# Latent scores begin with the latents' own tile and their weighing is spread; in the 16-head attention a key item goes ahead of the turned maxima, and ScalarE issues four of the key moves

## The reference, cut to what matters

```python
# L1 and L2: 16 heads of 8, one batch element at a time (L1 with biases and a mask on the 1500 keys)
scores = einsum('bhqd,bhkd->bhqk', q, k) / sqrt(8)
out = einsum('bhqk,bhkd->bhqd', softmax(scores), v) @ Wo.T
# L3: 8 heads of 64; keys and values come from the context AND the 56 latents
kv = concatenate([layer_norm(context), layer_norm(latents)], axis=1) @ Wkv     # 1500 + 56 rows
sim = einsum('bhid,bhjd->bhij', l2norm(q) * q_scale, l2norm(k) * k_scale) * 8
sim = where(mask, sim, max_neg)                # the mask is on the 1500 context rows alone
out = layer_norm(einsum('bhij,bhjd->bhid', softmax(sim), v) @ Wo)
```

## Time and profile before

| what | us |
|---|---|
| median of three executions | 4443.74 |
| lowest and highest of them | 4441.89, 4443.81 |
| the profiled execution, its own time | 4445.88 |
| its span, first to last instruction | 4443.8 |
| TensorE busy in the span | 3737.9 |
| VectorE, ScalarE, GpSimd busy | 2632.0, 2039.1, 1119.3 |

### The profile page before, as it was taken

One profiled execution on the slowest core, in us unless ns is written; L12 is line 12 of the kernel. 1 busy time (PEld: TensorE's weight loads), 2 busy tenths in 40 slices (PEclk: granted clock), 3 DMA queues, 4 the chain that ended last, 5 costly groups with the idle time before them and its releaser, 6 DMA issues. The chain is left out here.

```text
span 4443.8 us, 97631 instructions
## 1 busy us (share of the span) xinstructions
PE 3737.9 (84%) x40750; PEld 2568.5 (58%) x40750; DVE 2632.0 (59%) x3696; ACT 2039.1 (46%) x3827; POOL 1119.3 (25%) x1043
## 2 busy tenths in 40 slices
PE   7789678888888799588888887255999999999988
PEld 4454357776777544377777775132666666666654
DVE  5634356666666233466666663433777777777751
ACT  3300035555555100255555553212777777777643
POOL 0000122222221100322222221200555555555530
PEclk8889889999999799799999998566999999999989
DMA  7800165555553000444444440000000000000000
GB/s 217 255 20 0 57 168 150 146 146 146 146 146 96 39 0 0 122 118 121 116 121 119 118 122 8 0 13 21 14 22 22 21 22 22 22 22 22 22 1 23
DMA packets 107986, 329.21 MB, mean 74 GB/s; under 512 B 54151, under 2 KB 55247, under 8 KB 107023
## 3 DMA queue, kind: packets, MB, share of 16 engines
q1 hardware_dynamic: 107567, 323.20, 27.2%
HBM read 168.20 MB, written 7.00 MB: 39 GB/s over the span
## 5 line engine op out<-in xcount | busy, mean ns | idle before, releaser
L1758 POOL TENSOR_TENSOR l_S<-l_S,l_shift 125x448 f32<-125x448 f32 (+1 forms) x416 | 461.1, 1143 | 278.4 <-ACT l_shift L1988 275.9
L1179 ACT ACTIVATE L2a_probs<-ps 125x448 f32<-125x448 f32 x768 | 383.2, 544 | 191.1 <-PE ps L1089 177.4
L1179 ACT ACTIVATE L1a_probs<-ps 125x448 f32<-125x448 f32 x768 | 383.3, 544 | 190.7 <-PE ps L1089 177.1
L1212 DVE TENSOR_REDUCE L2a_chunk_max<-ps 112x1 f32<-112x1000 f32 x256 | 300.8, 1197 | 166.8 <-PE ps L1052 166.4
L1212 DVE TENSOR_REDUCE L1a_chunk_max<-ps 112x1 f32<-112x1000 f32 x256 | 300.8, 1197 | 159.0 <-PE ps L1052 158.4
L1969 ACT ACTIVATE ctx_stats<-ps 125x512 f32<-125x512 f32 (+1 forms) x416 | 248.0, 596 | 216.6 <-PE ps L1816 205.4
L1867 PE MATMUL ps<-l_S,l_z 125*128 125x448 f32 x768 | 342.7, 543 | 0.0
L2059 DVE SCALAR_TENSOR_TENSOR l_S<-ps,l_neg_cols,l_inv_norms 125x448 f32<-125x448 f32 x384 | 258.5, 681 | 117.1 <-PE ps L1836 116.0
L2034 DVE TENSOR_REDUCE l_norms<-ctx_stats 125x8 f32<-125x512 f32 (+1 forms) x416 | 268.9, 676 | 82.6 <-ACT ctx_stats L1969 82.2
L1052 PE MATMUL ps<-L1a_keys,L1a_queries 98*112 98x500 f32 x768 | 261.8, 423 | 55.9 <-DVE L1a_k_full L1199 22.0
L1089 PE MATMUL ps<-L1a_queries,L1a_keys 100*125 100x224 f32 x1536 | 307.1, 299 | 0.4 <-ACT L1a_probs L1179 0.4
(11 more groups left out here) (407 smaller groups left out, 7646.8 us busy)
## 6 DMA issues: line engine op xcount, KB each, us to landing
L1a_keys<-L1a_k_hi SPq DMA_DIRECT2D x256, 187.5 KB
L2a_keys<-L2a_k_hi SPq DMA_DIRECT2D x256, 187.5 KB, 3.7
a_ctx_T<-in_ctx_T SPq DMA_DIRECT2D x32, 750.0 KB, 11.2
xn<-L_valid SPq DMA_DIRECT2D x32, 750.0 KB, 7.8
L1a_ctx_T<-in_ctx_T SPq DMA_DIRECT2D x32, 750.0 KB, 6.2
L1a_keys<-L1a_k_lo SPq DMA_DIRECT2D x128, 187.5 KB
L2a_ctx_T<-in_ctx_T SPq DMA_DIRECT2D x32, 750.0 KB, 6.5
L2a_keys<-L2a_k_lo SPq DMA_DIRECT2D x128, 187.5 KB, 4.1
```

Of the source, the lines that this page charges most:

```text
L1179: nc.scalar.activation(probs[t % NPR][:, h * HQ // 2:(h + 1) * HQ // 2], s.ps[0:KP, i % 3, 0:HQ // 2], ACT.Exp).then_inc(probs_made, 1)
L1212: ins = nc.vector.tensor_reduce(chunk_max[:, n, 0:1], product, AX.XY, ALU.max)
L1758: nc.gpsimd.tensor_tensor(S[b % 2][0:r, t, :], S[b % 2][0:r, t, :], shift[0:r, :], ALU.add)\
```

## The change

The diff, cut to its core:

```diff
@@ attention_16_heads
-    step_items[10] += [("turn", 1, 0), ("keys", 3, 0)]
-    step_items[11].append(("keys", 3, 1))
+    step_items[10].append(("keys", 3, 0))
+    step_items[11] += [("turn", 1, 0), ("keys", 3, 1)]
@@ move_keys, SyncE
-                sp.wait_ge(k_lo_made, b * 2 + 2)
-                for g in range(G):
-                    sp.dma_start(keys[b % NKB][GR:2 * GR, g, :].bitcast(F32),
-                                 k_lo[g * GR:(g + 1) * GR, :].bitcast(F32)).then_inc(keys_moved, 16)
+                if b < 2:
+                    sp.wait_ge(k_lo_made, b * 2 + 2)
+                    for g in range(G):
...
@@ ScalarE
+            def move_remainders(b):
+                if b >= NKB:
+                    act.wait_ge(scores_made, (b - NKB + 1) * KT * 2)
+                act.wait_ge(k_lo_made, b * 2 + 2)
+                for g in range(G):
+                    act.dma_start(keys[b % NKB][GR:2 * GR, g, :].bitcast(F32),
+                                  k_lo[g * GR:(g + 1) * GR, :].bitcast(F32)).then_inc(keys_moved, 16)
...
+                    if t == 1 and b + 2 < B:
+                        move_remainders(b + 2)
@@ attention_latents, TensorE
+        SCORED = [KT] + list(range(KT))
...
-                for t in range(T):
+                for i in range(T):
                     if b + 1 < B:
-                        score_product(b + 1, t)
-                    if b >= 0 and t + LEAD < KT:
-                        weigh(b, t + LEAD)
+                        score_product(b + 1, i)
+                    later = [LEAD + (i + k) * (KT - LEAD) // T for k in range(2)]
+                    if b >= 0 and later[1] > later[0]:
+                        weigh(b, later[0])
@@ attention_latents, VectorE
+            def raise_by_latents(b):
+                dve.wait_ge(topped, b * NTOP + 2)
+                nc.vector.tensor_tensor(top[0:SQ, 1, :], top[0:SQ, 1, :], S[b % 2][0:SQ, KT, :], ALU.max).then_inc(topped, 1)
+
             def join_tops(b):
-                dve.wait_ge(S_made, b * T + T)
-                dve.wait_ge(topped, b * NTOP + NTOP - 2)
-                nc.vector.tensor_tensor(top[0:SQ, 1, :], top[0:SQ, 1, :], S[b % 2][0:SQ, KT, :], ALU.max).then_inc(topped, 1)
                 dve.wait_ge(topped, b * NTOP + NTOP - 1)
...
-                    for t in range(T):
-                        scale_scores(b + 1, t)
-                        if t == 1 and b >= 1:
+                    for i in range(T):
+                        if i == KT and b + 2 < B:
+                            center_latents(b + 2)
+                        scale_scores(b + 1, i)
+                        if i == 1 and b >= 1:
                             take_output(b - 1)
-                        if t == 11 and b + 2 < B:
-                            center_latents(b + 2)
-                        if t >= 4 and t % 2 == 0:
-                            raise_top(b + 1, t - 2)
+                        if i >= 5 and i % 2 == 1:
+                            raise_top(b + 1, i - 3)
+                        if i == 8:
+                            raise_by_latents(b + 1)
+                    raise_top(b + 1, KT - 2)
                     join_tops(b + 1)
```

More of the change, by code:

```diff
@@ L949, in move_keys @@
                                      k_hi[g * GR:(g + 1) * GR, :].bitcast(F32)).then_inc(keys_moved, 16)
-                sp.wait_ge(k_lo_made, b * 2 + 2)
-                for g in range(G):
-                    sp.dma_start(keys[b % NKB][GR:2 * GR, g, :].bitcast(F32),
-                                 k_lo[g * GR:(g + 1) * GR, :].bitcast(F32)).then_inc(keys_moved, 16)
+                if b < 2:
+                    sp.wait_ge(k_lo_made, b * 2 + 2)
+                    for g in range(G):
+                        sp.dma_start(keys[b % NKB][GR:2 * GR, g, :].bitcast(F32),
+                                     k_lo[g * GR:(g + 1) * GR, :].bitcast(F32)).then_inc(keys_moved, 16)
             def move_maxima(b):
@@ L1714, in attention_latents @@
         NTOP = KT // 2 + 1
+        RAISED = {2: 0, 4: 1, 6: 3, 8: 4, 10: 5}
+        SCORED = [KT] + list(range(KT))
         def rows(t):
@@ L1826, in queries_through_keys, with score_product @@
                 mm.then_inc(G_made, 1)
-            def score_product(b, t):
-                if t == 0:
+            def score_product(b, i):
+                t = SCORED[i]
+                if i == 0:
                     pe.wait_ge(G_lo_made, b + 1)
-                if b * T + t >= 2:
-                    pe.wait_ge(S_made, b * T + max(t - 1, 0))
-                out = s.ps[0:rows(t), 2 + t % 2, 0:HQ3]
+                if b * T + i >= 2:
+                    pe.wait_ge(S_made, b * T + max(i - 1, 0))
+                out = s.ps[0:rows(t), 2 + i % 2, 0:HQ3]
                 nc.tensor.matmul(out, tile_of(b, t, 0), G_hi[:, :], start=True, stop=False)
@@ L1925, in _ @@
                             project_out(b - 1)
-                for t in range(T):
+                for i in range(T):
                     if b + 1 < B:
-                        score_product(b + 1, t)
-                    if b >= 0 and t + LEAD < KT:
-                        weigh(b, t + LEAD)
-                    if b + 2 < B and 7 <= t < 7 + NG:
-                        turn_context(b + 2, t - 7)
-                    elif b + 2 < B and t == 7 + NG:
+                        score_product(b + 1, i)
+                    later = [LEAD + (i + k) * (KT - LEAD) // T for k in range(2)]
+                    if b >= 0 and later[1] > later[0]:
+                        weigh(b, later[0])
+                    if b + 2 < B and 7 <= i < 7 + NG:
+                        turn_context(b + 2, i - 7)
+                    elif b + 2 < B and i == 7 + NG:
                         turn_latents(b + 2)
@@ L2047, in take_queries_lo, with scale_scores @@
                     .then_inc(G_lo_made, 1)
-            def scale_scores(b, t):
+            def scale_scores(b, i):
+                t = SCORED[i]
                 r = rows(t)
-                dve.wait_ge(raw_made, b * T + t + 1)
-                if t == 0 and b >= 2:
+                dve.wait_ge(raw_made, b * T + i + 1)
+                if i == 0 and b >= 2:
                     dve.wait_ge(sums_made, b - 1)
                 heads_of = (S[b % 2][0:r, t, :].rearrange("p (h q) -> p h q", h=H8),
-                            s.ps[0:r, 2 + t % 2, 0:HQ3].rearrange("p (h q) -> p h q", h=H8))
+                            s.ps[0:r, 2 + i % 2, 0:HQ3].rearrange("p (h q) -> p h q", h=H8))
                 factors = bcast(inv_norms[0:r, t, :], SQ, 2)
```

4 lines of the change are left out of this document (2 added, 2 removed).

## The result

The changed kernel takes 4603.68 us (median of four, 4595.62 to 4608.14), the kernel before 4443.77 beside it: a ratio of 1.0358 [1.0340, 1.0376], 160 us slower. The prediction said 4407, at most 4470. The profiled execution's own time is 4601.7 us, its span 4599.9.

What follows compares the result with a forecast made beforehand. The prediction took TensorE's work plus its waits to bound a batch. From 4445.9 us it took 17 for steps 1 and 2 in both stages and 20 for the latents: 4409, or 4407 at the median; range 4370 to 4470.

Steps and rivals of the forecast that it cites:

- Step 1: L1 and L2: key item ahead of the turned maxima removes 1.80 us of TensorE waits a batch, 54.9 us a stage.
- All three waits: TensorE in L1: 1.36 us for `max_col`, 0.17 for `k_full`, 0.27 at the values for exponentials; all taken as gone.
- The cost of the late copy of the maxima: SyncE's copy of two maxima rows for the next batch: costed at nothing; if cover is short, 0.5 us a batch.
- Step 2: Four issues on ScalarE behind `L1a_v`'s start: 2.52 us, a new TensorE wait of 1.54 us, 46 us a stage.
- rival C: ScalarE, L1 and L2: none of the issues lies under `L1a_v`, 0.9 us more in 60 batches, 4462 us; chance 0.12.
- rival B: End of step 1: each issue costs ScalarE what remainders cost SyncE, 3.5 us for four, 4466 us; chance 0.20.
- A filled gap is worth its own length: TensorE: granted clock 1.00 and 0.99 in the windows read, so it already runs at its 2.4 GHz level.
- Step 3: Latents' score phase: merge taken out of the chain, turned maxima 0.67 us earlier a batch, 20 us in thirty batches.
- The new wait for z: Latents: the first context turn comes up before ScalarE ends `z`, so TensorE waits some 0.6 us.
- the join wait: Latents: TensorE's turned maxima wait for the join, said to shrink from 2.24 to about 1.3 us.
- the chain that I had named: Latents: weighing of the latents releases centring, then last pair maxima, join and turned maxima; said to still decide.
- B, C and both: Slower rivals: B 4466 us, chance 0.20; C 4462 us, chance 0.12; both together 4520 us, chance 0.04.

Runs made afterwards that it cites:

- the item order alone: The kernel before with only the first key item moved ahead of the turned maxima, all moves still issued by SyncE: 4326.44 us, ratio 0.9745.
- the kernel with the wait filled: The changed kernel with eleven idle 64-column products on TensorE ahead of the second half of step 3: 4471.64 us, ratio 1.0061.
- the kernel with one a step: The changed kernel with ScalarE's four issues set apart, one at the end of each of steps 1 to 4: 4348.45 us, ratio 0.9793.
- the kernel a step later: The changed kernel with ScalarE's four issues at the end of step 2 instead of step 1: 4465.19 us, ratio 1.0049.
- the third buffer: Both new orders, all moves issued by SyncE, and three buffers of centred latents instead of two: 4284.27 us, ratio 0.9648.
- SyncE behind: The changed kernel, but SyncE begins its eight moves only when the scores of step 2 are made: 4528.1 us, ratio 1.0205.
- ahead of the values: The changed kernel with the four issues in step 1 ahead of the emptying of the values, not behind it: 4456.24 us, ratio 1.0025.

## Why the prediction was wrong

**Step 1, the key item ahead: right.** Forecast -54.9 us a stage; the stages of the item order alone are 800.5 and 799.4 us, 56.6 and 57.6 below. All three waits went. The cost of the late copy of the maxima, put at nothing, shows in a few batches only.

**Step 2, the issues: the place and the path right, the size of one term wrong.** "I take 2.52 us, since ScalarE's queue is empty when it begins": the queue was empty, the DMA engines were not. Four issues measured 3.47 us in the median in L1 and 3.74 in L2. The rest of the step held: the issues begin beside `L1a_v` (rival C fell), and TensorE's wait is their length less about 1.0, forecast as 2.52 to 1.54, measured as 2.44 to 1.44, 3.16 to 2.14 and 3.20 to 2.18. So the term that failed is the 2.52 us for four issues; its right size is the one of rival B, which had 3.5 us, 4466 us for the kernel; the kernel with the wait filled, which has B's hold and no clock loss, took 4471.64. The price of an issue behind eight others was there, and I took the row of the first four instead. The rule that I set beside B, from the Trainium skill (Perfetto Trace Analysis, DMA Instruction — HWDGE), that the shared descriptor generator's lock lies inside the recorded instruction, fits the issues that grew on both engines where both issued, but those had full DMA engines too. It doesn't explain the long ones while SyncE was silent, nor the short ones beside SyncE's (0.51 us in the kernel with one a step).

**A term that was missing: the granted clock.** "A filled gap is worth its own length" was read from stretches at clock 1.00 and 0.99, and I let it hold for the stretch with the new wait too. The L1 of before had waits of 1.4 us and kept its clock; with waits of 2.0 to 3.2 us in all but two of its 60 batches, the changed kernel was at half speed for a stretch in 56 of them. Length alone doesn't decide it: four batches with waits of 2.0 to 2.8 us had none, the latents of before waited 2.24 us a batch at clock 0.99, and in L1 of the kernel a step later, where seven of the 13 stretches at half speed lie at the stops amid the values, four others lie behind waits of only 0.9 to 1.5 us. What decides it stays open. This term is 132 us, and without it the result would have been 4472, just outside the range. The Trainium skill (TensorE: Matmul & The Clock Gate, HAM oscillation) describes a loop in which one wait in every round drops the clock each time. The traces agree with that pattern: a fall in nearly every batch, and none between 700 and 1400 us with the wait filled. By the Trainium skill the waits in that loop are some 3 to 5 us; here 2.0 to 3.2 us were enough.

**Step 3, the latents: right.** Forecast -0.67 us a batch and 20 us; measured 37.52 to 36.93 a batch, and for the part alone 17 us by the medians side by side (4440.57 and 4423.33), 20 by the ratio of 0.9956, 23 by its stage (1184.3 to 1161.4). The new wait for z is 0.65 us (forecast 0.6), the join wait 1.2 (forecast 1.3), and the third buffer showed the chain that I had named. Two figures beside the forecast were slips: without the wait for `z` the bound is 0.67 + 0.57 = 1.24 us a batch, 37 us, and not 1.5 and 45; and slower was given 0.32, though B, C and both add up to 0.36. Neither touches the outcome.

**The sum.** Forecast: 4443.8 - 110 + 93 - 20 = 4407. Measured: -114 (4326.44 against the 4440.57 of before beside it), -17, +161 for the hold and +132 for the clock: 4443.8 - 114 - 17 + 161 + 132 = 4606, where the result is 4603.7. The last two are differences taken from that result, so the sum tests only that the two gains add up.

## What to carry to other kernels

A DMA issue is an instruction of the engine that makes it, with a length that depends on the transfers in flight and on how soon it follows the last issue: price it by a row in which as many transfers are in flight, not by the first ones of a burst, and if a busy engine has to issue, set the issues apart (here one a step, 0.51 to 0.78 us each, instead of four in 3.47). Compare its length with the slack between that engine and the one that waits for it, since all beyond comes back on the path. And when an edit makes one wait longer in every round, ask what the granted clock does after a wait of that length there: if no wait of that stage is as long, carry the fall to half speed as a rival with a price of its own.

## What the hardware showed unexpectedly

- One wait of TensorE in a batch of 27 us was enough to bring the clock down, though not every time. Waits of 1.4 us (the kernel before) left it at 1.00; with about 2.1 us (SyncE behind, and ahead of the values) it was 0.96 and 0.97, mostly at half for 3.4 us, in a quarter to seven tenths of the batches; with 2.0 to 3.2 us (the changed kernel) 0.90, at half for 6.8 us in most batches. And 2.24 us in a batch of the latents left it at 0.99. In batches with the same wait (SyncE behind), 3.4 us at half speed cost about 1.6 us and 6.8 us about 3.1.
- Eleven idle products of 64 columns in place of the wait kept the clock at 1.00 and made the kernel 132 us faster, although they compute nothing.
- Issues of the same transfers took 1.80 us for three begun on idle DMA engines, 2.97 us for three on full ones, and 0.51 us each, on full ones and beside SyncE's, with a pause of about half a microsecond or more before them.
- TensorE stopped for up to 2.3 us amid the values, often in two kernels and rarely in others, with no semaphore that it waited for. Each of the 68 stops over 0.3 us in the two ended 1.2 to 1.7 us after a 16 KiB transfer of kind "instruction".
